# A longer loop body for the edge groups of a graph network: 44 groups per iteration in place of 16

## The chip, the cores and the metric

The kernel runs on one core of one Trainium2 chip. The metric is device time in microseconds (us) of one execution. TensorE (PE), VectorE (DVE), ScalarE (ACT), GpSimd (POOL) and SyncE (SP) each run their own instruction stream, with semaphores between them, and each stream is written with its own copy of the loops below.

## The reference

A graph with 2500 nodes of 128 features and 82500 edges, sorted by destination, passes through six layers of a SchNet-like network and then three GIN layers:

```python
for l in range(6):                                   # first network
    W = ssp(edge_attr @ mlp_w1[l] + mlp_b1[l]) @ mlp_w2[l] + mlp_b2[l]
    W = W * C[:, None]                               # C: cosine cutoff of the edge length
    msg = (h @ conv_w1[l])[src] * W
    agg = segment_sum(msg, dst, num_segments=N)
    h = h + (ssp(agg @ conv_w2[l] + conv_b2[l]) @ lin_w[l] + lin_b[l])
x = layernorm(x + h)
for l in range(3):                                   # second network, with x as h
    z = (1 + eps[l]) * h + segment_sum(h[src], dst)
    h = relu(z @ W1[l] + b1[l]) @ W2[l] + b2[l]
out = layernorm(x + h)
```

All in float32; `ssp(x) = softplus(x) - log 2`.

## The kernel before, in words

Edges are put into 176 groups of 512 (4 tiles of 128). A first part, up to about 1070 us, permutes and transposes the edge records once. Then come the six layers. A layer is `Fori(0, NIT)` with NIT = 11 iterations, and the body of an iteration holds U = 16 groups, written out. On each engine the body is a software pipeline over steps `i`:

- PE at step i: first edge product of group i (L787, `ps_h`); selection of the source rows of group i-2 (L686, `ps_g`, named `ps_a` in the rows) and its second product (L696, `ps_w`); one tile of the neighbour counts that the second network needs (L715); the aggregation of group i-4 (L706, `ps_a`), which waits until DVE has added group i-5 into `aggT`.
- DVE at step i: adds group i-5 into its windows of `aggT` (L1456, four instructions, one after the other), multiplies the message of group i-3 (L1463), finishes the softplus of group i (L1585), and does its share of a count tile (L1495, L1496, L1509).
- ACT at step i: exponential and logarithm of group i (L1075, L1077), copies the selected rows of group i-2 (L1035) and seeds the product bank of group i-1 (L1039).
- POOL: for each group four one-hot matrices (L589, `phot`), two groups behind the aggregation. At the start of an iteration it copies the indices of the whole body (L604, L605).
- SP issues the two DMA loads of a group (`attr`, `select`) four groups ahead.

The steps of a group i-5 to i-1 of an iteration reach back into the groups of the iteration before, so the pipeline doesn't drain between iterations; at steps under 5 this part stands in `If(it > 0)`. Only after the last iteration of a layer a few extra steps drain it, and `late_chunks` updates the nodes.

Nodes are updated in five chunks of 512. `aggT` is complete for a chunk before the layer ends, because edges are sorted by destination, so three chunks are updated early, in iterations EARLY_AT = [5, 8, 9]: the table `early_now` says in which iteration which chunk stands, each engine loads its entry at the start of an iteration (`load_early`, L427), and the parts of the update stand in `If(early_step > 0)` at steps 0 to 3 (PE L720, L725, L731; DVE L1515, L1520, L1528; ACT L1022, L1024, L1029). The other two chunks follow in `late_chunks`.

COUNT_STEP gives the steps at which a count tile is done: 3 to 14, which is BT = 12 tiles in an iteration, or 792 in all; the counts share the banks `ps_t` with the early chunks. `Uses` keeps the registers that the waits compare with.

Of the kernel before, what the change touches and what calls it, by code (L numbers as in the profile page):

```python
# [23 lines left out]
P = 128  # L24
# [16 lines left out]
CHUNKS = 3  # L41
# [12 lines left out]
AS = M  # L54
BG = -(-REAL // (L0 * NIT))
BT = BG * TPG
# [31 lines left out]
ADD_LAG = 6  # L88
COUNT_MAX = 255
# [15 lines left out]

COUNT_STEP = list(range(3, 15))
assert len(COUNT_STEP) == BT


def chunk_of(g):  # L110
    return max(k for k in range(CHUNKS) if GROUP_FIRST[k] <= g)


def gnn_program(nc, xT_d, srcc_d, dst_d, plan_d, ew_d, rec_d, edge_w_d, b2_d, first_w_d, node_w_d, gin_w_d,
# [9 lines left out]
    with ExitStack() as ctx:  # L124
# [25 lines left out]

        early_now = sb("early_now", [P, NIT], i32)
        slack = sb("slack", [P, 1])
# [88 lines left out]
        tile_after = spare[:, 0:PTC * (BLOCKS - 1) // 2 + 1].bitcast(bf16)  # L241
        pends, plan = spare[:, 4 * GE:4 * GE + 2 * PT], spare[:, 7 * GE:7 * GE + NG + NIT]
        assert 2 * PT <= 3 * GE and NG + NIT <= GE
        prel_now = sb("prel_now", [P, U * TPG])
# [168 lines left out]
        def turned_after(r):  # L413
# [11 lines left out]

        def load_early(eng, it, least=0):
            return eng.value_load(early_now[0:1, bass.ds(it, 1)], min_val=least, max_val=EARLY)  # L427

# [200 lines left out]
        def _(pe):  # L629
# [147 lines left out]
            with pe.Fori(0, L0) as layer:  # L777
                prime(layer)
                with pe.Fori(0, K) as k:
                    with pe.Fori(0, NIT) as it:  # L780
                        uses = Uses(pe, layer * (K * NIT) + k * NIT + it).ready(-1, -5)
                        early_step = load_early(pe, it)
                        for i in range(U):
                            if i == 0:
                                uses.wait_attr(i)
                                uses.wait(ssp_done, i - 2)
                            pe.matmul(ps_h[i % 2][:, :], edge_w[0:G1, EW_W1:EW_W1 + F], attr[:, i % AS, :],  # L787
                                      start=True, stop=True).then_inc(mm1_done[i % M], 1)
                            if i >= 2:
                                second_product(uses, it, i - 2, layer)  # L790
                            else:
                                with pe.If(it > 0):
                                    second_product(uses, it, i - 2, layer)
                                if i == 1:
                                    with pe.If(k * NIT + it < 1):
                                        keep_turning(FILL_FIRST)
                            if i == 3:
                                with pe.If(early_step > 0):
                                    chunk_project(layer * NCH + load_early(pe, it, 1))
                            for q in tiles_at(i - 1):  # L800
                                count_tile(uses, q)
                            if i + 1 < U:
                                uses.wait_attr(i + 1)
                                uses.wait(ssp_done, i - 1)
                            if i >= 4:
                                aggregate(uses, i - 4)
                            else:
                                with pe.If(it > 0):
                                    aggregate(uses, i - 4)
                            if i == 0:  # L810
                                with pe.If(early_step > 0):
                                    early = load_early(pe, it, 1)
                                    pe.wait_ge(node_w_in, layer * 16 + 16)
                                    uses.wait(add_done, -1 - ADD_LAG)
                                    uses.wait_count(count_added[TPG - 1], -1)
                                    chunk_prod1(pe.snap(early * CH - CH), layer * NCH + early)
                            if i == 2:
                                with pe.If(early_step > 0):
                                    chunk_prod2(layer * NCH + load_early(pe, it, 1))
                    uses = Uses(pe, layer * (K * NIT) + k * NIT + (NIT - 1))  # L820
# [153 lines left out]
        def _(act):  # L974
# [80 lines left out]
            with act.Fori(0, L0) as layer:  # L1055
# [4 lines left out]
                with act.Fori(0, K) as k:  # L1060
                    with act.Fori(0, NIT) as it:
                        uses = Uses(act, layer * (K * NIT) + k * NIT + it)
                        uses.ready(-1, -5)
                        early_step = load_early(act, it)
                        for u in range(U):
                            if u == 1:
                                with act.If(early_step > 0):
                                    chunk_softplus(layer * NCH + load_early(act, it, 1))
                            if u == 3:
                                with act.If(early_step > 0):  # L1070
                                    early = load_early(act, it, 1)
                                    chunk_store(act.snap(early - 1), layer * NCH + early,
                                                act.snap((layer * EARLY + early + (EARLY - 1)) * 16), next_half)
# [119 lines left out]
        def _(dve):  # L1193
# [215 lines left out]
            for g in range(GROUP_FIRST[CHUNKS - 1], GROUPS):  # L1409
# [18 lines left out]
            steps.sync()  # L1428
            dve.tensor_scalar(early_now[:, :], plan[:, NG:NG + NIT], sorted_dst[:, :], None, ALU.mult
                              ).then_inc(early_set, 1)  # L1430
# [126 lines left out]
            with dve.Fori(0, L0) as layer:  # L1557
# [4 lines left out]
                with dve.Fori(0, K) as k:  # L1562
# [4 lines left out]
                    with dve.Fori(0, NIT) as it:  # L1567
# [3 lines left out]
                        counted = dve.snap(layer * NIT + it)  # L1571
                        early_step = load_early(dve, it)
                        for i in range(U):
                            if i >= 5:
                                add_window(uses, i - 5, it)
# [5 lines left out]
                            if i >= 3:  # L1581
# [5 lines left out]
                                                     ).then_inc(ssp_done[i % M], 1)  # L1587
                            if i == 0:
                                with dve.If(early_step > 0):
                                    chunk_clamp(layer * NCH + load_early(dve, it, 1))  # L1590
                            if i == 1:
                                with dve.If(early_step > 0):
                                    chunk_ssp(layer * NCH + load_early(dve, it, 1))
                            if i == 2:
                                with dve.If(early_step > 0):
                                    early = load_early(dve, it, 1)
                                    chunk_h(dve.snap(early * CH - CH), layer * NCH + early)
                                window_ready(layer * K + k)
# [174 lines left out]
```

## Time and profile before

| what | value |
|---|---|
| median of 3 runs | 5893.71 us (5890.15 to 5894.4) |
| the profiled execution's own time | 5894.77 us |
| its span, first to last instruction | 5893.1 us |
| mean granted TensorE clock | 0.919 |
| busy: PE, DVE, ACT, POOL | 83%, 60%, 47%, 68% |

Times in the rows count from the start of the span. A digit of the engine rows is the busy share of a slice of 147 us in tenths. The layers fill the slices 8 to 38, and in these PE is nearly always busy; the second network follows after 5560 us.

### The profile page before, as it was taken

Reading aid. Unit: us, or ns where it says so; the run is one execution under the profiler, and the core shown is the slowest. Engines: PE = TensorE matmul, PEld = TensorE weight load, DVE = VectorE, ACT = ScalarE, POOL = GpSimd, SP = SyncE. Lnnn points to the kernel's source line nnn. Section 1 sums busy time; section 2 is a strip of 40 time slices with the busy share of each in tenths; the row PEclk is TensorE's granted clock in tenths of the full one; section 3 lists DMA queues with packets and bytes.
Section 4 is the critical chain, followed back from the end, with each engine's and each line's share of the span. In section 5 each row is a group of like instructions: output and inputs, shape, how many; then the busy total and the mean of one; then the engine's idle time right before and its main releaser. Section 6 shows DMA issues by size and latency. Waiting matters only on the chain.

```text
span 5893.1 us, 130525 instructions
## 1 busy us (share of the span) xinstructions
PE 4903.4 (83%) x33026; PEld 3993.5 (68%) x33041; DVE 3560.8 (60%) x10645; ACT 2777.2 (47%) x4801; POOL 4011.3 (68%) x5030
## 2 busy tenths in 40 slices
PE   1036446899999999999998999999999999999999
PEld 0035446777777777777777777877778777777644
DVE  8412224576666766667676666766667667666522
ACT  0012223455555555555555555555555555555422
POOL 4777773577776777767777677776777767777500
PEclk5567778999999999999999999999999999999999
DMA  8258667533333333333333333434333343333200
GB/s 344 77 167 277 213 218 242 165 123 117 119 119 119 124 119 118 119 120 123 120 122 116 119 120 119 124 117 120 121 119 122 117 122 123 118 121 118 90 2 10
DMA packets 431082, 778.19 MB, mean 132 GB/s; under 512 B 55099, under 2 KB 115973, under 8 KB 427349
## 3 DMA queue, kind: packets, MB, share of 16 engines
q1 hardware_dynamic: 388108, 728.55, 38.9%
q0 software_dynamic: 20640, 34.39, 1.8%
q10 hardware_dynamic: 21928, 11.64, 0.7%
q14 instruction: 371, 3.03, 0.2%
q8 instruction: 35, 0.57, 0.0%
HBM read 605.57 MB, written 168.79 MB: 131 GB/s over the span
## 4 chain that ended last, share of the span: by engine, by line
PE 57%; issue 13%; POOL 11%; DVE 9%; DVEq 6%; DMA 1%; ACT 1%; SPq 1%; ACTq 0%; POOLq 0%
PE ps_a L706 14%; PE ps_a L686 12%; PE ps_w L696 12%; PE ps_h L787 12%; POOL permuted L571 11%; DVE aggT L1456 6%; DVEq L333 3%; PE ps_pair L905 3%; DVEq L1456 1%; DVE src_hot L1495 1%; DVEq L427 1%; DVE hid L1585 1%; DVEq L1509 1%; PE ps_pair L720 1%; DVE counts L1509 1%
## 5 line engine op out<-in xcount | busy, mean ns | idle before, releaser
L589 POOL TENSOR_SCALAR phot<-pwin_now,prel_now,pcut_now 128x128 f32<-128x128 f32 x4224 | 3298.7, 796 | 1021.2 <-PE ps_a L706 985.6
L1456 DVE TENSOR_TENSOR aggT<-aggT,ps_a 128x128 f32 x4224 | 1212.8, 287 | 888.0 <-issue 367.0
L686 PEld LDWEIGHTS ps_a<-hi_mid,buffers 128*128 128x128 f32 x8448 | 1127.7, 195 | 575.8 <-issue 575.1
L706 PE MATMUL ps_a<-phot,ex_msg 128*128 128x128 f32 x8448 | 1204.7, 287 | 276.7 <-DVE aggT L1456 276.0
L706 PEld LDWEIGHTS ps_a<-phot,ex_msg 128*128 128x128 f32 x8448 | 1053.9, 196 | 342.0 <-issue 330.5
L1075 ACT ACTIVATE xc<-ps_h 128x512 f32<-128x512 f32 x1056 | 630.4, 597 | 1278.3 <-PE ps_h L787 1265.1
L686 PE MATMUL ps_a<-hi_mid,buffers 128*128 x8448 | 1143.2, 279 | 30.7 <-ACT hid L1035 27.9
L787 PE MATMUL ps_h<-buffers,edge_w 112*128 112x512 f32 x2112 | 1136.7, 621 | 7.7 <-DVE hid L1585 7.7
L696 PE MATMUL ps_w<-edge_w,hid 128*128 128x128 f32 x8448 | 1120.3, 276 | 0.0
L696 PEld LDWEIGHTS ps_w<-edge_w,hid 128*128 128x128 f32 x8448 | 1034.4, 193 | 0.0
L1585 DVE SCALAR_TENSOR_TENSOR hid<-xc,ps_h 128x512 f32<-128x512 f32 x1056 | 722.8, 684 | 335.7 <-PE ps_w L696 267.9
L571 POOL DMA_INDIRECT permuted<-counts x645 | 653.8, 1014 | 248.4 <-issue 195.9
L1039 ACT COPY ps_w<-seed_rows 128x512 f32<-128x512 f32 x1056 | 624.4, 591 | 398.0 <-DVE ex_msg L1463 395.5
L1077 ACT ACTIVATE xc<-xc,half_col 128x512 f32<-128x512 f32 x1056 | 762.3, 722 | 34.7
L1463 DVE TENSOR_TENSOR ex_msg<-ps_w,hid 128x512 f32<-128x512 f32 x1056 | 721.8, 684 | 12.0 <-issue 11.7
L1035 ACT COPY hid<-ps_a 128x512 f32<-128x512 f32 x1056 | 598.7, 567 | 26.5 <-PE ps_a L686 26.3
L668 PE MATMUL ps_h<-ident_lane,hid 128*104 128x128 f32 x1408 | 217.4, 304 | 459.6 <-DMA hid<-permuted 459.3
L668 PEld LDWEIGHTS ps_h<-ident_lane,hid 128*104 128x104 f32 x1408 | 187.7, 191 | 476.2 <-DMA hid<-permuted 289.8
L787 PEld LDWEIGHTS ps_h<-buffers,edge_w 112*128 112x128 f32 x2112 | 336.6, 198 | 48.6 <-issue 42.5
L1016 ACT COPY ex_msg<-ps_h 104x512 f32<-104x512 f32 x88 | 51.6, 586 | 586.8 <-PE ps_w L672 586.8
L1395 DVE COPY buffers<-hid 128x4 f32<-128x4 f32 x176 | 43.4, 246 | 422.5 <-DMA hid<-permuted 408.4
L1509 DVE TENSOR_TENSOR counts<-counts,ps_pair 128x128 f32 x792 | 223.6, 282 | 61.6 <-issue 61.4
(236 smaller groups left out, 2875.6 us busy)
## 6 DMA issues: line engine op xcount, KB each, us to landing
buffers<-src_select SPq DMA_DIRECT2D x1056, 256.0 KB, 2.8
buffers<-attr_permuted SPq DMA_DIRECT2D x1056, 224.0 KB, 2.8
hid<-permuted SPq DMA_DIRECT2D x176, 208.0 KB, 4.3
counts<-in_rec SPq DMA_DIRECT2D x19, 1404.0 KB, 9.9
permuted<-aggT SPq DMA_DIRECT2D x26, 944.0 KB, 26.8
src_select<-ex_msg SPq DMA_DIRECT2D x88, 256.0 KB, 4.8
src_select<-buffers SPq DMA_DIRECT2D x88, 256.0 KB
attr_permuted<-ex_msg SPq DMA_DIRECT2D x88, 224.0 KB, 3.6
```

Source lines behind the costliest of these rows:

```text
L571: pool.indirect_dma_start(out=perm_d[:, :], out_offset=bass.IndirectOffsetOnAxis(ap=pos_i[:, t:t + 1], axis=0), in_=rec[:, r % RING, t - P ...
L589: op = pool.tensor_scalar(phot[:, u % 2, t, :], pwin_now[:, :], prel_now[:, u * TPG + t:u * TPG + t + 1], pcut_now[:, u * TPG + t:u * TPG ...
L686: mm = pe.matmul(ps_g[:, t * F:(t + 1) * F], select[:, u % AS, t * P:(t + 1) * P], table[:, bass.ds(starts[t], F)], start=True, stop=True)
L696: mm = pe.matmul(ps_w[u % 2][:, t * F:(t + 1) * F], hid[:, u % 2, t * P:(t + 1) * P], edge_w[:, EW_W2:EW_W2 + F], start=False, stop=(t == ...
L706: mm = pe.matmul(ps_a[:, t * PWIN:(t + 1) * PWIN], msg[:, u % 2, t * F:(t + 1) * F], phot[:, u % 2, t, :], start=True, stop=True)
L787: pe.matmul(ps_h[i % 2][:, :], edge_w[0:G1, EW_W1:EW_W1 + F], attr[:, i % AS, :], start=True, stop=True).then_inc(mm1_done[i % M], 1)
L1039: act.copy(ps_w[v % 2][:, :].rearrange("p (t f) -> p t f", f=F), seed_rows[:, :].unsqueeze(1).broadcast_to([P, TPG, F])).then_inc(seeded[v ...
L1075: act.activation(xc[:, u % 2, :], ps_h[u % 2][:, :], ACT.Exp).then_inc(exp_done, 1)
L1077: act.activation(xc[:, u % 2, :], xc[:, u % 2, :], ACT.Ln, bias=half_col[:, :]).then_inc(log_done, 1)
L1456: dve.tensor_tensor(window, window, ps_a[:, t * PWIN:(t + 1) * PWIN], ALU.add).then_inc(part_added[t] if t < TPG - 1 else add_done[u % M], 1)
L1463: dve.tensor_tensor(msg[:, u % 2, :], ps_w[u % 2][:, :], picked[:, u % 2, :], ALU.mult).then_inc(msg_done[u % M], 1)
L1585: dve.scalar_tensor_tensor(out=hid[:, i % 2, :], in0=xc[:, i % 2, :], scalar=LOG_MAX, in1=ps_h[i % 2][:, :], op0=ALU.min, op1=ALU.max).the ...
```

## The change

The body holds 44 groups and a layer has 4 iterations: 176 groups as before. What hangs on these two numbers:

- Iterations in the whole program: 24 in place of 66. POOL's copies of the indices are 176 columns wide in place of 64.
- The early chunks stand at "spots", one at step 0 and one at step 22 of the body (SPOT = 22), so a layer has 8 of them. EARLY_AT becomes [3, 6, 7]: chunk 0 at step 22 of iteration 1, chunk 1 at step 0 of iteration 3, chunk 2 at step 22 of iteration 3; that is at the groups 66, 132 and 154 of the layer, where it was 80, 128 and 144. PE, DVE and ACT load their entry of `early_now` at each spot.
- The count tiles stand at the steps 4 to 21 and 26 to 39: 32 in an iteration, 768 in all. A layer's padding of tiles is smaller (NG 192 in place of 198).

```diff
-U = 16
+U = 44
-NIT = 11
+NIT = 4
-BG = -(-REAL // (L0 * NIT))
+BG = -(-GROUPS // (L0 * NIT))
-EARLY_AT = [5, 8, 9]
+SPOT = 22
+SPOTS = U // SPOT
+EARLY_AT = [min(s for s in range(NIT * SPOTS) if chunk_of(max(0, s * SPOT - ADD_LAG)) >= k) + n for k, n in ((1, 0), (2, 0), (2, 1))]
-COUNT_STEP = list(range(3, 15))
+COUNT_STEP = [step for step in range(U) if 4 <= step % SPOT and step < U - 1][:BT]
...
-        early_now = sb("early_now", [P, NIT], i32)
+        early_now = sb("early_now", [P, NIT * SPOTS], i32)
...
+        def counted_until(step):
+            return sum(at < step for at in COUNT_STEP) // TPG
...
 (PE; DVE and ACT in the same way)
-                        early_step = load_early(pe, it)
                         for i in range(U):
+                            if i % SPOT == 0:
+                                spot = pe.snap(it * SPOTS + i // SPOT)
+                                early_step = load_early(pe, spot)
...
-                            if i == 3:
+                            if i % SPOT == 3:
                                 with pe.If(early_step > 0):
-                                    chunk_project(layer * NCH + load_early(pe, it, 1))
+                                    chunk_project(layer * NCH + load_early(pe, spot, 1))
...
-                            if i == 0:
+                            if i % SPOT == 0:
                                 with pe.If(early_step > 0):
...
-                                    uses.wait(add_done, -1 - ADD_LAG)
-                                    uses.wait_count(count_added[TPG - 1], -1)
+                                    uses.wait(add_done, i - 1 - ADD_LAG)
+                                    uses.wait_count(count_added[TPG - 1], counted_until(i) - 1)
...
-                            if i == 2:
+                            if i % SPOT == 2:
```

## Rows read from the trace of the kernel before

**Rows 1.** The page: span, busy times, PE and its clock by slices.
```profile
span 5893.1 us, 130525 instructions
PE 4903.4 (83%) x33026; PEld 3993.5 (68%) x33041; DVE 3560.8 (60%) x10645; ACT 2777.2 (47%) x4801; POOL 4011.3 (68%) x5030
...
PE   1036446899999999999998999999999999999999
...
PEclk5567778999999999999999999999999999999999
```

**Rows 2.** Windows, third layer, iterations: length, busy (count) per engine, PEclk, DMA.
```profile
2697.75:2762.80 65.05, 60.52 (x429) 51.34 (x428) 45.19 (x135) 37.11 (x64) 50.38 (x66) 0.97 0.39 122
...
3027.88:3092.81 64.93, 60.69 (x430) 51.29 (x429) 45.20 (x135) 37.22 (x64) 50.38 (x66) 0.97 0.39 122
3092.81:3162.85 70.04, 63.98 (x441) 52.64 (x441) 47.76 (x139) 38.95 (x67) 50.40 (x66) 0.98 0.38 117
```

**Rows 3.** Windows inside the iteration at 3027.88, from group to group.
```profile
3027.88:3035.60 7.72, 3.99 (x27) 3.17 (x27) 2.36 (x7) 2.29 (x4) 3.12 (x4) 1.00 0.42 129
3035.60:3040.79 5.19, 5.19 (x29) 4.16 (x27) 2.44 (x7) 2.49 (x5) 3.12 (x4) 0.68 0.01 2
3040.79:3044.33 3.54, 3.54 (x29) 3.06 (x27) 2.51 (x9) 2.28 (x4) 3.12 (x4) 1.00 0.43 139
...
3047.87:3051.51 3.64, 3.64 (x29) 3.15 (x28) 2.92 (x10) 2.28 (x4) 3.64 (x5) 1.00 0.43 135
3051.51:3055.54 4.03, 3.83 (x29) 3.15 (x28) 2.87 (x9) 2.27 (x4) 3.23 (x5) 1.00 0.37 126
```

**Rows 4.** Chain that ended last, the same boundary: start, us, what.
```profile
3027.96 3.18 issue
3031.13 0.06 DVEq L1567
```

**Rows 5.** Timeline, the same boundary: start, us, what [idle before <-releaser].
```profile
3032.93 1.55 DVE L1456 TENSOR_TENSOR aggT<-aggT,ps_a 128x128 f32 x4 [4.97 <-issue]
...
3034.62 1.19 PE L706 MATMUL ps_a<-phot,ex_msg 128*128 128x128 f32 x8 [3.73 <-DVE aggT L1456]
3035.60 1.92 PE L787 MATMUL ps_h<-buffers,edge_w 112*128 112x512 f32 x2
...
3040.79 1.02 PE L787 MATMUL ps_h<-buffers,edge_w 112*128 112x512 f32 x2
```

**Rows 6.** DMA queues in the gap 3027.5:3031.1: packets, MB, share.
```profile
q14 instruction: 1, 0.01, 0.5%
```

**Rows 7.** DMA queues, 680:1064 (first part, no loops).
```profile
q8 instruction: 14, 0.23, 0.2%
```

**Rows 8.** DMA queues, 1070.66:1133.6, the first iteration of the first layer.
```profile
q8 instruction: 5, 0.08, 0.6%
```

**Rows 9.** DMA queues, 1830:5560, layers two to six: every instruction packet.
```profile
q14 instruction: 279, 2.29, 0.2%
```

**Rows 10.** Windows: straight code of 680:1064; eleven groups of layers one and three.
```profile
680.00:1064.00 384.00, 234.24 (x1688) 211.63 (x1688) 138.51 (x761) 113.83 (x212) 206.70 (x201) 0.82 0.75 245
...
1092.18:1133.60 41.42, 40.85 (x300) 34.68 (x298) 32.49 (x100) 25.50 (x44) 34.36 (x44) 1.00 0.41 132
2588.10:2629.50 41.40, 40.86 (x300) 34.88 (x299) 32.08 (x98) 26.20 (x46) 32.26 (x42) 1.00 0.43 133
```

**Rows 11.** Timeline, an early chunk at an iteration's start.
```profile
3171.21 1.92 PE L720 MATMUL ps_pair<-aggT,node_w 128*128 x2
...
3181.47 1.07 PE L725 MATMUL ps_pair<-ex_msg,node_w 128*128 128x512 f32 x2
```

**Rows 12.** Loads of the early entry, line 427: ns min/median/max.
```profile
L427 PEldq TENSOR_LOAD <-early_now x126: 308/313/674, 1067.4 to 5557.9; - x126
```

**Rows 13.** Timeline, POOL after the boundary at 3027.88.
```profile
3045.39 4.68 POOL L589 TENSOR_SCALAR phot<-pwin_now,prel_now,pcut_now 128x128 f32<-128x128 f32 x6 [0.44 <-POOL pcut_now L605]
```

**Rows 14.** Timeline, DVE at the second layer's start.
```profile
1831.27 0.15 DVE L1559 TENSOR_SCALAR cb_ln<-node_w 128x1 f32<-128x1 f32 x1 [5.73 <-DMA node_w<-in_node_w]
```

More of the change, by code:

```diff
@@ L81, with chunk_of @@
 STEP_PRIME = 5
-EARLY_AT = [5, 8, 9]
+ADD_LAG = 6
+def chunk_of(g):
+    return max(k for k in range(CHUNKS) if GROUP_FIRST[k] <= g)
+SPOT = 22
+SPOTS = U // SPOT
+assert SPOTS * SPOT == U
+EARLY_AT = [min(s for s in range(NIT * SPOTS) if chunk_of(max(0, s * SPOT - ADD_LAG)) >= k) + n for k, n in ((1, 0), (2, 0), (2, 1))]
 EARLY = len(EARLY_AT)
@@ L1063, in _ @@
                         uses.ready(-1, -5)
-                        early_step = load_early(act, it)
                         for u in range(U):
-                            if u == 1:
+                            if u % SPOT == 0:
+                                spot = act.snap(it * SPOTS + u // SPOT)
+                                early_step = load_early(act, spot)
+                            if u % SPOT == 1:
                                 with act.If(early_step > 0):
-                                    chunk_softplus(layer * NCH + load_early(act, it, 1))
-                            if u == 3:
+                                    chunk_softplus(layer * NCH + load_early(act, spot, 1))
+                            if u % SPOT == 3:
                                 with act.If(early_step > 0):
-                                    early = load_early(act, it, 1)
+                                    early = load_early(act, spot, 1)
                                     chunk_store(act.snap(early - 1), layer * NCH + early,
@@ L1428, in _ @@
             steps.sync()
-            dve.tensor_scalar(early_now[:, :], plan[:, NG:NG + NIT], sorted_dst[:, :], None, ALU.mult
+            dve.tensor_scalar(early_now[:, :], plan[:, NG:NG + NIT * SPOTS], sorted_dst[:, :], None, ALU.mult
                               ).then_inc(early_set, 1)
@@ L1587, in _ @@
                                                      ).then_inc(ssp_done[i % M], 1)
-                            if i == 0:
+                            if i % SPOT == 0:
                                 with dve.If(early_step > 0):
-                                    chunk_clamp(layer * NCH + load_early(dve, it, 1))
-                            if i == 1:
+                                    chunk_clamp(layer * NCH + load_early(dve, spot, 1))
+                            if i % SPOT == 1:
                                 with dve.If(early_step > 0):
-                                    chunk_ssp(layer * NCH + load_early(dve, it, 1))
+                                    chunk_ssp(layer * NCH + load_early(dve, spot, 1))
+                            if i % SPOT == 2:
+                                with dve.If(early_step > 0):
+                                    early = load_early(dve, spot, 1)
+                                    chunk_h(dve.snap(early * CH - CH), layer * NCH + early)
                             if i == 2:
-                                with dve.If(early_step > 0):
-                                    early = load_early(dve, it, 1)
-                                    chunk_h(dve.snap(early * CH - CH), layer * NCH + early)
                                 window_ready(layer * K + k)
@@ L1739 @@
     rec = np.ascontiguousarray(attr.reshape(EACH, P, REC).transpose(1, 0, 2))
-    plan = np.zeros((P, NG + NIT), np.float32)
-    for c, it in enumerate(EARLY_AT):
-        plan[:, TILE_FIRST[chunk_of(it * U - ADD_LAG)] // TPG:NG] = (c + 1) * CH
-        plan[:, NG + it] = c + 1
+    plan = np.zeros((P, NG + NIT * SPOTS), np.float32)
+    for c, spot in enumerate(EARLY_AT):
+        plan[:, TILE_FIRST[chunk_of(spot * SPOT - ADD_LAG)] // TPG:NG] = (c + 1) * CH
+        plan[:, NG + spot] = c + 1
     w1 = np.zeros((L0, P, F), np.float32)
```

19 lines of the change are left out of this document (9 added, 10 removed).

## The prediction

> **What bounds the kernel now.** I read the page first [rows 1]. PE is at 9 tenths or more in all slices of the six layers, at nearly its full clock, so a layer ends when PE has done its groups. Then I cut one layer into iterations [rows 2]. An iteration without an early chunk takes 65.05 or 64.93 us and PE is busy for 60.5 to 60.7 us of it: some 4 us are lost somewhere. The windows from group to group [rows 3] say where. In steady state a group takes 3.54 us, 3.64 us with a count tile, and 4.03 us at every fourth count tile, where DVE also loads the places of the next four. These windows are filled by PE. Only the first two groups of the body are long: 7.72 and 5.19 us.
>
> The chain of waits [rows 4] and the timeline [rows 5] show why. DVE's loop branch (L1567) is followed by 3.18 us in which its sequencer does nothing that is recorded; its next work, the addition of the last group but four into `aggT`, starts 4.97 us after its last instruction. PE waits 3.73 us for that addition before L706. Afterwards PE runs its next matmuls slower: the pair L787 takes 1.92 us in place of 1.02, and the granted clock of that window is 0.68, which is a mix of the two levels 2.4 and 1.2 GHz; in the idle time before, it was still granted 1.00 [rows 3, 5]. So a boundary costs PE twice, by the wait and by a slow stretch behind it. In the gap lies exactly one instruction packet of queue q14 [rows 6]: DVE is fetching code.
>
> The Trainium skill ("Runtime: NRT & Kernel Launch", Instruction fetch mechanics) says that a taken branch out of the loaded window forces a fetch before execution goes on. By that rule, the trace agrees.
>
> **What a boundary costs, and what goes.** Sixteen steady groups would take 16 x 3.54 = 56.6, plus 12 x 0.10 for count tiles = 1.2, plus 3 x 0.38 for the places = 1.1: 59.0 us. The iteration takes 64.9 to 65.0, so a boundary costs 5.9 us; by the other way, 7.72 + 5.19 - 2 x 3.54 = 5.8 [rows 3]. I take 5.8. A layer has 10 boundaries now and 3 afterwards: 7 x 6 = 42 go, 42 x 5.8 = 243.6 us. Nothing else is late in its place in mid-body: POOL needs 3.12 us a group and DVE is busy 2.51 us of 3.54 [rows 3]. The price stays the same at the 18 that remain, as far as DVE makes it; others are below.
>
> **Count tiles.** 792 become 768: 24 x 0.10 + 6 x 0.38 = 4.7 us less, since each stands on PE's or DVE's full path [rows 3]. No end far away: nothing to 5 us.
>
> **Early chunks.** At a boundary one costs 70.04 - 65.0 = 5.0 to 5.5 us [rows 2]. In it PE's own work is three products: the first took 1.92 us at the slow clock, the second 1.07 at full clock [rows 11], the third is of the same size as one of a group's, 0.9. At full clock that is 2.9 us, the lower bound at mid-body. The rest is DVE, which takes four more instructions of 512 columns and at a body's step 3 already starts counting. At step 22 PE comes in at full clock, and the first count tile stands at step 26, a step later than now. I take 4.2 there, between 2.9 and 5.5. Of 18 chunks 12 move to a mid-body spot: 12 x 1.2 = 14 us less; the 6 at a boundary gain 0.4 each from the later count tile, 2 us. Together 16 us less, between 0 and 36.
>
> **What the mid-body spots add.** At step 22 PE, DVE and ACT each load an entry: 313 ns on PE's sequencer [rows 12] and some ALU work and branches, 0.6 to 0.7 us together. They are no engine work; PE's sequencer loads four starts for each group in the same way and the group still takes 3.54 us. DVE has over 1 us of air at steps 22 to 25, which have no count tile. Twelve spots without a chunk at 0.3 us: 4 us; bounds 0 and, where all of it shows, 0.7 x 24 = 17 us.
>
> **POOL's copies.** 176 columns in place of 64, on an engine that sits idle at the boundary anyway: POOL starts its first new group at 3045.39 [rows 13], 3.12 us of work, and PE wants it near the end of step 4, at about 3050.5 (step 5 starts at 3051.51 and an aggregation takes 1 us) [rows 3]. That is 2 us of air; nothing.
>
> **Code fetch of the longer body, the one thing that grows.** Queue q8 brings PE's code: 14 packets in straight code in which PE ran 1688 matmuls and as many weight loads [rows 7, 10], so 241 of these per packet of 16 KB. In the first iteration of the first layer it brings 5 [rows 8], and in the layers two to six none at all [rows 9]: the only instruction packets there are q14's. So PE's whole layer is resident now. The new body has 429 x 2 x 44/16 = 2360 such instructions, 10 packets, and with the sequencer's own some 12. Whether that still fits no row shows.
>
> (The skill's same section gives PE's instruction memory as 128 KiB or 2048 instructions. By it the new body does not fit, and PE must fetch at each loop branch as DVE does; this speaks against the change.)
>
> Since no row decides it, I take the dearer case, not fitting, from PE's side with DVE's price. First, fetching in a straight line: in the first layer's first iteration PE received its packets while it ran; eleven groups there took 41.42 us, the same eleven in the third layer, without a fetch, 41.40 [rows 10]. So it costs nothing. Second, the loop branch: if PE loses what DVE loses, 3.2 us or, as its packets are twice as long, 4 us, its first three products of the new body (2.9 us at full clock) start 4 us later, at 3032. They end at 3035 to 3036.5, where L706 starts at 3034.62 now [rows 5]; the slow stretch that follows today would lie in front. So the two fetches overlap nearly whole. I add 0.5 us for each of 18 boundaries, 9 us, bounds 0 and 3.5 each (63). ACT's body grows likewise; it has over 1 us of idle time in every group and its first product of the new body comes from PE. SP issues its loads four groups ahead, 14 us. At a layer's start DVE waits 5.73 us for the node weights [rows 14], and PE's branch lies under it: 0.5 us x 6 = 3, bounds 0 and 3 each (18).
>
> **Sum.** -243.6 - 4.7 - 16 + 4 + 9 + 3 = -248 us against the profiled execution's own 5894.8 us (1.1 us over the median): 5646.5; against the median of 5893.7, **5645 us**. Preparation and second network stay.
>
> **The rivals.**
> - *Fetches add up* (18%): PE, ACT or POOL come back from the loop branch later than DVE, and L706 waits for PE's own products or, further on, for `phot`. For it: four engines now leave their loaded window at once, and POOL's air is 2 us only. Against: the overlap above. With 3 us more at 18 boundaries and 1 at each layer: 5645 + 60 = 5705.
> - *The mid-body spot stalls like a boundary* (5%): the skip over the early block leaves DVE's window. For it: nothing but the price of 5.8 us; against: three such skips at steps 0 to 2 stand in every iteration now and steps 2 and 3 take 3.54. 24 x 5.8 = 139: 5784.
> - *The other side: PE's straight fetch doesn't keep up* (4%). Twelve packets in each of 24 iterations, 288 in all, and a packet takes 0.6% x 62.9 us x 16 engines / 5 = 1.2 us of an engine [rows 8]. If PE stood still for each, 288 x 1.2 = 346 us: 5990, slower than before. It decides from 0.86 us per packet. Against: the two equal stretches of rows 10.
> - *It doesn't do what it says* (2%): the 5.8 us belong to something that comes every 16 groups, not to the branch. For it nothing; at 5895.
> - The forecast: 71%, its own range 5610 to 5690.
>
> Faster than 5882 (0.2%, about what can be told from no change): 71 + 18 + 5 = 94%, same 2%, slower 4%. The range: below, early chunks at the bound and no price for PE's branch give 5645 - 20 - 12 = 5613, and a cheaper boundary 5605; above, it takes in the first rival with its bound, 5720.
>
> **What would show it.** In the profile after, six layers of 3 boundaries each: iterations of about 168 us (44 x 3.54 + 32 x 0.10 + 8 x 0.38 = 162.0, plus 5.8). L706's wait for L1456 falls to under half. Queue q8 has some 250 packets more, spread over the layers, and steady groups still take 3.54 and 3.64 us; if they take longer, the third rival is right. The window over step 0 and 1 tells the first rival: over 15 us in place of 12.9, with PE's own sequencer late. A gap at step 22 of an iteration without a chunk tells the second. The forecast is wrong if the boundaries that are left cost over 9 us each, or if the groups lose 0.1 us each (106 us in all).

## The result, and the profile after

| | before | after |
|---|---|---|
| median | 5893.79 us (4 runs) | 5767.03 us (5763.99 to 5768.43, 4 runs) |
| ratio | 1 | 0.9785, 95% interval 0.9772 to 0.9799 |
| preparation, to the first product of layer one | 1070.7 us | 1076.3 us |
| six layers, each from its first to its last group's first product (L787, after: L797) | 4319.1 us | 4145.1 us |
| five transitions between these | 153.3 us | 195.9 us |
| what follows | 350.1 us | 349.3 us |

The change is worth 127 us, half of the 248 that were forecast. The layers give 174 us; the transitions take back 43. The 5.6 us more of preparation lie wholly ahead of the layers: PE enters its layer loop at 1072.1 us in place of 1066.6. In the runs below on chips with this preparation, PE enters it between 1065.3 and 1071.7 us, in no order of the body's length, so no run puts these 5.6 us down to the change.

The page after, with the busy times and the queues that carry instructions (packets, MB, share):

```profile
span 5766.7 us, 127153 instructions
...
PE 4825.2 (84%) x33002; PEld 3960.9 (69%) x33017; DVE 3537.8 (61%) x10489; ACT 2763.3 (48%) x4801; POOL 3985.2 (69%) x4946
...
q8 instruction: 374, 6.13, 0.4%
q14 instruction: 403, 3.30, 0.2%
```

Queue q8, PE's code, had 35 packets in the page of before. It now has 374, and in layers two to six, where there was none [rows 9]:

```profile
q8 instruction: 283, 4.64, 0.5%
q14 instruction: 301, 2.47, 0.3%
```

The layer is cut again from each group's first product to the next one's, and a group is called by its step in the body. Windows of the third layer (length, busy and count of PE, PEld, DVE, ACT, POOL, then PEclk, DMA share, GB/s): three iterations; the two windows of a boundary and the group behind it; step 22 without an early chunk; step 22 with one:

```profile
2535.08:2703.32 168.24, 159.79 (x1126) 132.90 (x1126) 116.85 (x342) 100.17 (x174) 131.18 (x170) 0.98 0.40 126
2703.32:2882.89 179.57, 168.96 (x1189) 143.09 (x1189) 126.21 (x367) 103.49 (x179) 137.46 (x178) 0.97 0.40 124
2882.89:3053.89 171.00, 162.58 (x1177) 138.80 (x1177) 123.80 (x364) 101.56 (x176) 137.48 (x178) 0.98 0.41 129
2694.08:2703.32 9.24, 3.51 (x26) 2.84 (x25) 3.31 (x9) 2.28 (x4) 6.22 (x8) 0.92 0.40 114
2703.32:2709.55 6.23, 6.22 (x26) 5.19 (x27) 1.57 (x3) 2.40 (x4) 0.00 (x0) 0.57 0.01 4
2709.55:2713.09 3.54, 3.54 (x28) 3.06 (x27) 2.38 (x6) 2.28 (x4) 3.11 (x4) 1.00 0.49 141
2965.79:2970.54 4.75, 3.83 (x29) 3.15 (x28) 2.87 (x9) 2.26 (x4) 3.11 (x4) 1.00 0.48 136
2787.20:2793.20 6.00, 4.96 (x32) 3.62 (x30) 2.96 (x9) 2.38 (x4) 3.97 (x6) 1.00 0.55 167
```

The steady group still takes 3.54 us, with q8's packets running beside it. The boundary takes 9.24 + 6.23 in place of 7.72 + 5.19 [rows 3]. Its long windows are now those of the old body's last group and the new body's first, one group earlier, since PE itself now stops, before the new body's first product. The timeline shows it (start, us, what, idle before and its releaser):

```profile
2702.12 1.55 DVE L1468 TENSOR_TENSOR aggT<-aggT,ps_a 128x128 f32 x4 [4.63 <-issue]
...
2703.32 2.08 PE L797 MATMUL ps_h<-buffers,edge_w 112*128 112x512 f32 x2 [5.73 <-issue]
...
2705.19 1.91 PE L694 MATMUL ps_a<-hi_mid,buffers 128*128 x8
...
2709.55 1.02 PE L797 MATMUL ps_h<-buffers,edge_w 112*128 112x512 f32 x2
```

DVE loses about what it lost before (4.63 us, 4.97 in [rows 5]). PE, which had lost only by waiting for DVE, now stands for 5.73 us, waits for nobody, and then runs its next 18 products at about half their pace (1.02 to 2.08, 1.05 to 1.91; clock 0.57 over the window). ACT and POOL wait for PE, and none of SP's loads is waited for.

PE's branches name the place. Durations of the iteration loop's branch and of the layer loop's branch (ns, minimum/median/maximum), in the kernel before:

```profile
L780 PEldq COMPARE_BRANCH  x66: 76/208/222, 1131.9 to 5545.2; - x66
L777 PEldq COMPARE_BRANCH  x6: 67/209/229, 1823.1 to 5570.4; - x6
```

and after:

```profile
L788 PEldq COMPARE_BRANCH  x24: 67/3454/3996, 1238.8 to 5419.4; - x24
L785 PEldq COMPARE_BRANCH  x6: 67/7166/7467, 1796.3 to 5445.3; - x6
```

A loop branch takes PE 3.5 us now, one back to the layer's start 7.2; both rows count the last branch of each loop too, which is not taken and lasts 0.07. As the median of the 18 boundaries, two packets of q8 start 1.0 and 4.6 us after the start of the branch, the branch ends 3.68 us after its start, and the first product comes another 3.57 us later: after the second packet.

The start of the third layer, with `prime` (PE's 16 small products that seed its banks for the first groups; L742, after: L750). Before, there was no idle time in front of it. Now there are 7.17 us; the end of DVE's wait [rows 14] is the second line, and PE's first edge product (L797) comes after it, where it came before it:

```profile
2531.38 3.77 PE L750 MATMUL ps_w<-b_row,ones_row 1*128 1x128 f32 x16 [7.17 <-issue]
...
2532.23 0.15 DVE L1571 TENSOR_SCALAR cb_ln<-node_w 128x1 f32<-128x1 f32 x1 [6.14 <-DMA node_w<-in_node_w]
...
2535.08 3.78 PE L797 MATMUL ps_h<-buffers,edge_w 112*128 112x512 f32 x4
```

And step 22 without a chunk, on DVE and PE:

```profile
2966.45 0.29 DVE L1521 TENSOR_TENSOR counts<-counts,ps_pair 128x128 f32 x1 [0.34 <-issue]
...
2967.88 1.55 DVE L1468 TENSOR_TENSOR aggT<-aggT,ps_a 128x128 f32 x4 [1.14 <-issue]
...
2969.58 1.13 PE L714 MATMUL ps_a<-phot,ex_msg 128*128 128x128 f32 x8 [0.92 <-DVE aggT L1468]
```

DVE's load of the spot's entry (2966.47 to 2967.23 on its sequencer) stands in the 1.14 us ahead of the addition that PE waits for. Just before it (2965.25 to 2966.07) DVE's sequencer has loaded the places of four count tiles.

### The profile page after: what moved, and what is told of

Same layout as the page of the kernel before. It is cut to its first block, busy times and chain, and to the rows that moved or that the text cites. A ratio compares the mean times of both kernels' runs of the same rounds, so it can differ in the third digit from the quotient of the medians.

```text
span 5766.7 us, 127153 instructions
## 1 busy us (share of the span) xinstructions
PE 4825.2 (84%) x33002; PEld 3960.9 (69%) x33017; DVE 3537.8 (61%) x10489; ACT 2763.3 (48%) x4801; POOL 3985.2 (69%) x4946
## 4 chain that ended last, share of the span: by engine, by line
PE 60%; issue 12%; POOL 11%; DVE 8%; DVEq 5%; ACT 1%; DMA 1%; SPq 1%; ACTq 0%; POOLq 0%
PE ps_a L714 14%; PE ps_a L694 13%; PE ps_w L704 13%; PE ps_h L797 13%; POOL permuted L579 11%; DVE aggT L1468 5%; PE ps_pair L915 3%; DVEq L338 3%; DVEq L1468 1%; DVE src_hot L1507 1%; DVE hid L1599 1%; DMA permuted<-aggT 1%; DVEq L1521 0%; POOL counts L586 0%; DVEq L435 0%
## 5 line engine op out<-in xcount | busy, mean ns | idle before, releaser
L714 PE MATMUL ps_a<-phot,ex_msg 128*128 128x128 f32 x8448 | 1175.9, 282 | 94.6 <-DVE aggT L1468 93.5
L797 PE MATMUL ps_h<-buffers,edge_w 112*128 112x512 f32 x2112 | 1111.7, 608 | 101.0 <-issue 100.9
L694 PE MATMUL ps_a<-hi_mid,buffers 128*128 x8448 | 1131.6, 277 | 29.9 <-ACT hid L1045 29.5
L714 PEld LDWEIGHTS ps_a<-phot,ex_msg 128*128 128x128 f32 x8448 | 1035.0, 193 | 149.1 <-issue 140.5
L797 PEld LDWEIGHTS ps_h<-buffers,edge_w 112*128 112x128 f32 x2112 | 330.6, 195 | 130.6 <-issue 129.8
```

Source lines behind the costliest of these rows:

```text
L694: mm = pe.matmul(ps_g[:, t * F:(t + 1) * F], select[:, u % AS, t * P:(t + 1) * P], table[:, bass.ds(starts[t], F)], start=True, stop=True)
L714: mm = pe.matmul(ps_a[:, t * PWIN:(t + 1) * PWIN], msg[:, u % 2, t * F:(t + 1) * F], phot[:, u % 2, t, :], start=True, stop=True)
```

## The experiments

Each has "layers", the sum of the six as in the table above (before 4319.1, after 4145.1), "transitions" (153.3 and 195.9), and the ratio to the kernel before in the same batch. The first four ran on a chip where the preparation took some 1335 us, so only ratios and these sums are compared. The sums, and all means of groups, come from one profiled execution of each kernel.

**Both entries at step 0.** Edit to the kernel after, on PE, ACT and DVE alike:

```diff
-                            if i % SPOT == 0:
-                                spot = pe.snap(it * SPOTS + i // SPOT)
-                                early_step = load_early(pe, spot)
+                            if i == 0:
+                                spots = [pe.snap(it * SPOTS + n) for n in range(SPOTS)]
+                                early_steps = [load_early(pe, at) for at in spots]
+                            spot, early_step = spots[i // SPOT], early_steps[i // SPOT]
```

> The changed kernel (44 groups in the body), but PE, DVE and ACT load both entries of early_now at step 0 of the body; the parts in the If blocks stay where they are. Theory: the 1.2 us that step 22 loses in every iteration (4.75 us in place of 3.54) is DVE's load of the entry, 0.8 us on its sequencer ahead of the addition that PE waits for; at step 0 it lies in the fetch gap. So 24 x 1.2 = 29 us less than the changed kernel's 5767: 5738, and the interval at step 22 back at 3.54 to 3.65. Rival: the loss is in the branches over the early parts, or in DVE's two places of the count tile there; then no change, 5767.

Measured: ratio 0.9751 [0.9734, 0.9767]; layers 4136.1, only 9 us less than after, where 29 were expected; transitions 190.3. Step 22 without a chunk falls from 4.75 to 4.00, first row here, but the boundary grows, its first window to 9.9 us in the median from 9.24:

```profile
3215.93:3219.93 4.00, 3.83 (x29) 3.15 (x28) 2.87 (x9) 2.27 (x4) 3.12 (x4) 1.00 0.37 126
...
2944.74:2954.27 9.53, 3.71 (x28) 3.04 (x27) 2.91 (x9) 2.28 (x4) 6.25 (x8) 0.93 0.43 111
```

So of the 1.21 us of step 22 the load is 0.75. The other 0.46 don't belong to the spot: the steps 6, 10 and 14 take 4.00 us as well, in this kernel and in the kernel after. Each of them, and step 22, holds the product of a count tile (3.65 in place of 3.54) and follows a DVE step in which the places of four tiles are loaded (0.35 more). At the boundary the second entry costs about 0.6 us (8.76 in place of 8.11 us over two steady groups, as a mean), so only 9 us of the 18 (24 x 0.75) stay gained.

**The loop's head shifted.** 64 waits that are long met, merged to 32 instructions, ahead of PE's layer loop, where they run once:

```diff
+            for _ in range(64):
+                pe.wait_ge(perm_kept, GROUPS)
```

> The changed kernel with 32 more instructions (waits that are already met) in PE's straight code ahead of the layer loop, run once. They move PE's loop body against the 16 KB packets of code. Theory: at each loop branch PE now waits for two packets one behind the other, because the body starts a few instructions before a packet's end (packets at 2696.9 and 2700.5, first product at 2703.3). Shifted, one packet is enough: the body's first product comes some 2.3 to 3.3 us earlier after the branch, 18 x 2.5 = 45 us less: 5722. The boundary (last and first interval, 9.2 + 5.9 us) falls from 8.1 us over two steady groups to 5.5 or so. Rival: the second wait is another thing (attr's load, a semaphore); no change but for 1 to 2 us more, 5769.

Measured: ratio 0.9715 [0.9699, 0.9731]; layers 4105.1, 40 us less; transitions 201.8. The same boundary:

```profile
2945.04:2952.38 7.34, 3.70 (x29) 3.04 (x27) 2.44 (x6) 2.28 (x4) 6.22 (x8) 1.00 0.46 143
2952.38:2957.65 5.27, 5.27 (x26) 4.54 (x27) 2.44 (x6) 2.40 (x4) 0.00 (x0) 0.68 0.01 2
```

The branch takes as long (median 3.72 us), the two packets come at the same moments after it (1.0 and 4.7 us), but the first product follows 1.34 us behind the branch in place of 3.57. The boundary costs 7.34 + 5.27 - 7.08 = 5.5 here. The boundaries without a chunk cost 5.5 and 6.1 us (means of the layers' first and of their second): the price of before. Nothing was changed but where PE's code lies in its packets. So the extra price of the 18 boundaries is the wait for the second packet. That the loop's head had only few instructions behind it in the first one is the reading that fits; no trace shows a packet's content.

**Longer bodies.** 88 groups x 2 and 176 x 1; no count tile stands at a spot's last step, and a layer has 120 of them in place of 128 (the padding rounds otherwise):

```diff
-U = 44
+U = 88        (second kernel: 176)
...
-NIT = 4
+NIT = 2        (second kernel: 1)
...
-COUNT_STEP = [step for step in range(U) if 4 <= step % SPOT and step < U - 1][:BT]
+COUNT_STEP = [step for step in range(U) if 4 <= step % SPOT < SPOT - 1][:BT]
```

> U = 88, NIT = 2 (one boundary in a layer in place of three), count tiles at steps 4 to 20 of each 22. Theory: 12 boundaries less than the changed kernel at 8.1 us each, 97 us; layer starts (PE's 7.5 us branch) and the four spots of a layer stay: 5767 - 97 = 5670. Rival (longer code costs in straight line too): at or over 5720.

> U = 176, NIT = 1: the body is the whole layer, no boundary inside. Theory: 18 boundaries less at 8.1 us, 146 us: 5767 - 146 = 5621; PE's branch at the layer's end still takes 7 to 8 us and all 8 spots of a layer still cost. Rival: something grows with the body (registers, fetch in straight line), at or over 5700.

Measured: 88 groups 0.9597 [0.9581, 0.9613], layers 4030.7, transitions 197.3; 176 groups 0.9462 [0.9446, 0.9478], layers 3948.9, transitions 198.9. The first step takes 12 boundaries away and 114 us, 9.4 of them by the 48 count tiles less, so 8.8 us each (a few spots cost less here as well, see "Blocks only where a chunk can be"); the second takes the last 6 and 82 us, 13.6 each, of which 9.4 are the boundary and the rest comes from the groups around it and the layers' first. The transitions do not grow with the body any more (195.9, 197.3, 198.9).

**Idle code behind a condition, first try.** In the 16 groups of the kernel before, with 36 idle instructions (`keep_turning`: products whose result nobody uses) and, in the second, 12:

```diff
+                            with pe.If(early_step > EARLY):
+                                keep_turning(36)        (second kernel: 12)
```

> The kernel before (16 groups, 11 iterations) with an If block of 36 filler matmuls in each step of PE's body, behind a condition that never holds (early_step > EARLY). Nothing of it runs; it only makes PE's body some 2300 instructions long, as the 44 groups do, all else as before. Theory: PE's body is no longer resident, so queue q8 brings code in every iteration (some 9 packets of 16 KB), PE's loop branch waits for it at 60 boundaries and at 5 layer starts. The boundary rises from 5.8 us to 7 to 8.5, a layer's start by 8 us: +70 to +160 and +45: 1.02 to 1.035 of before. Steady groups stay at 3.54 and 3.65. Rival (what grew in the change is not PE's code but the longer body's other work): same time as before, q8 silent.

> As b1_pe_code_2300, with 12 fillers in each block: PE's body is some 1600 instructions, the layer's code with its ends some 2300. Theory: the body stays resident within a layer, the layer's start does not: boundaries as before (5.8 us), layer transitions longer by 8 us each: +45 us, 1.007 of before. q8 some 3 to 9 packets a layer. Rival: a body that fits keeps all: 1.000.

Measured: 1.0003 [0.9994, 1.0013] and 1.0005 [0.9996, 1.0015]. That tells nothing of the theory: q8 brought 35 packets in all, as many as before, so PE's program had its old length. The condition lies outside the value's declared range, and the compiler must have dropped the blocks.

**A short body.** The kernel before with 8 groups x 22, two count tiles a step at steps 3 to 6:

```diff
-U = 16
+U = 8
...
-NIT = 11
+NIT = 22
...
-EARLY_AT = [5, 8, 9]
+EARLY_AT = [9, 16, 17]
...
-COUNT_STEP = list(range(3, 15))
+COUNT_STEP = [3, 3, 4, 4, 5, 5, 6, 6]
```

> The kernel before with U = 8, NIT = 22: eight groups in the body, 21 boundaries in a layer, early chunks in iterations 9, 16 and 17, count tiles two at a step at steps 3 to 6 (1056 tiles). DVE's body is half as long. Theory: a boundary's 5.8 us are DVE's code fetch; half the body is at most two or three packets of 8 KB and stays, q14 falls silent within the layers, a boundary costs 1 to 2 us. 126 x 1.5 in place of 60 x 5.8, and 264 count tiles more at 0.2: 190 - 348 + 53 = -105 us: 0.982 of before. Rival (the branch itself, or the pipeline's refill, costs): 66 x 5.8 + 53 = +436 us, 1.07.

Measured: 1.042 [1.0403, 1.0438], layers 4539.7; 0.982 was expected. First group, steady group, a group with two tiles, last group:

```profile
3033.51:3038.09 4.58, 3.98 (x26) 3.15 (x27) 2.31 (x7) 2.27 (x4) 2.68 (x4) 1.00 0.04 12
3038.09:3041.63 3.54, 3.54 (x28) 3.06 (x27) 2.46 (x7) 2.40 (x5) 3.13 (x4) 1.00 0.34 128
...
3052.42:3057.04 4.62, 3.89 (x31) 3.25 (x29) 3.50 (x14) 2.33 (x5) 3.29 (x4) 1.00 0.45 131
3061.79:3067.25 5.46, 4.05 (x30) 3.22 (x28) 4.08 (x15) 2.49 (x5) 3.70 (x5) 1.00 0.40 128
```

Queue q14, DVE's code, from 1900 to 5500 us:

```profile
q14 instruction: 20, 0.16, 0.0%
```

It had 269 packets in the same stretch of before. So DVE's body of 8 groups stays loaded, and the boundary costs 1.04 us, at most 1.9 if all that the last group has over a group with two tiles is its too, in place of 5.8. The branch and the pipeline's refill are still there, and q14's packets and most of the price are gone: the 5.8 us are the fetch of DVE's code, and behind it PE's start at the slow clock. The kernel is slower for another reason, which the expectation had at 0.2 us a tile: two tiles in a group cost up to 1.1 us, five times what two groups with one tile pay.

**The next entry loaded early.** The kernel of 176 groups, with each spot's entry loaded 18 steps ahead:

```diff
+                            if i % SPOT == 4 and i + SPOT < U + 4:
+                                next_spot = pe.snap(it * SPOTS + i // SPOT + 1)
+                                next_step = load_early(pe, next_spot)
```

> U = 176, NIT = 1 with the entry of the next spot loaded at step 4 of each 22, so no load stands at a spot. Theory: 42 spots in mid-body lose 0.75 us less each, as the first experiment on the entries gave (4.75 to 4.00): 31 us less than a4_u176, 0.5% of before: 0.941. Rival: the load only costs elsewhere, 0.946.

Measured: 0.9449 [0.9433, 0.9464], 5563.02 us; layers 3944.9. The layers take four us less than with the load in its place, where 31 were expected: step 22 lost its 0.7 us, other groups gained 0.3 to 0.5. The rival is right.

**PE's code alone made longer.** The kernel before, with blocks that never run but can't be dropped; DVE's, ACT's and POOL's code is untouched:

```diff
+                            with pe.If(K > 2):
+                                keep_turning(36)        (second kernel: 12)
```

> The kernel before (bodies of 16 groups, 11 iterations), with 36 idle TensorE instructions behind a condition on K that is never met at run time in each of the 16 groups of the body: they are in the program and never run. PE's body then has about as many instructions as the body of 44 groups (some 2300), while DVE's, ACT's and POOL's stay as they were. Theory (PE's code no longer stays loaded, and it pays at each taken branch, in two packets of q8 at a loop branch): q8 brings packets in all six layers, a boundary costs 7 to 8.5 us in place of 5.8 (60 of them: +70 to +160) and each layer's start 8 us more (5 of them and the first, +40): ratio 1.02 to 1.035. Rival (the dearer boundary of the long body comes from DVE's, ACT's or POOL's longer code): 0.998 to 1.003, even if q8 brings packets. If the skips themselves cost, the steady group is over 3.54 us and tells it.

> The same with 12 idle instructions behind the condition in each group in place of 36: PE's loop body grows by about 200 to 400 instructions and may still fit, while body, layer's start and layer's end together are longer than in the kernel before. Theory: layers are entered at the dear price if q8 brings packets there (5 to 6 times 8 us: +45, ratio 1.007) and boundaries stay at 5.8 us. Rival: all still stays loaded, no q8 packets in layers two to six, ratio 0.999 to 1.001.

Measured with 36: 1.03 [1.0283, 1.0317]; layers 4441.4, 122 us more than before, which is 2.0 for each of 60 boundaries; transitions 199.3, 46 more. The steady group stays at 3.54, so skipping the blocks costs nothing. The branch of the iteration loop, q8 in layers two to six, and a boundary with the group behind it:

```profile
L780 PEldq COMPARE_BRANCH  x66: 76/3548/3986, 1131.8 to 5714.6; - x66
```

```profile
q8 instruction: 590, 9.67, 1.1%
```

```profile
2827.68:2836.68 9.00, 3.81 (x29) 3.13 (x27) 3.19 (x11) 2.28 (x4) 6.25 (x8) 1.00 0.40 115
2836.68:2841.97 5.29, 5.29 (x26) 4.26 (x27) 2.25 (x6) 2.40 (x4) 0.00 (x0) 0.68 0.01 3
2841.97:2845.51 3.54, 3.54 (x28) 3.06 (x27) 2.37 (x6) 2.29 (x4) 3.12 (x4) 1.00 0.40 146
```

Measured with 12: 1.0074 [1.0057, 1.0091]; layers 4314.5, not above before; transitions 200.6, 47 more. Its loop branch, q8, and what PE waits for at the third layer's start:

```profile
L780 PEldq COMPARE_BRANCH  x66: 76/208/212, 1132.0 to 5589.5; - x66
```

```profile
q8 instruction: 45, 0.74, 0.1%
```

```profile
PE ps_w L742 <- issue: 7.8, 1, 7.8
```

Both effects of the change are here, each by itself, in the kernel before and with no other engine's code touched. With 36 the body no longer stays loaded: boundaries go from 5.92 to 7.97 us, and layer starts up by 9 us (the branch of the layer loop takes 8.2 us as the median of five). With 12 the body stays, the way from a layer's end to its start does not: q8's 45 packets lie at the layers' ends, at their starts and in their first 50 us, and only the 9 us at the starts are paid. The rival, another engine's code, is out for both.

**Blocks only where a chunk can be.** 176 groups, entry loads and conditions at spots 3, 6 and 7 alone:

```diff
+def has_early(i, step):
+    return i % SPOT == step and (NIT > 1 or i // SPOT in EARLY_AT)
...
-                            if i % SPOT == 0:
+                            if has_early(i, 0):
```

> The body of a whole layer (176 groups, 1 iteration), in which the entry loads and the blocks of an early chunk stand only at the three spots that have one, in place of all eight. Theory: a spot without a chunk costs 0.75 us for the load and 0.3 us for the skips where the steps are full; five such spots in each of six layers go: 15 to 30 us less in the layers than with all eight (3948.9 us over the six layers, ratio 0.946), ratio 0.941 to 0.944. Rival: with a load that meets slack further on the cost moves and does not go: within 6 us of 3948.9.

Measured: 0.9448 [0.9433, 0.9464]; layers 3945.3. The rival is right. Of the five spots taken away three (0, 22, 110) had cost 0.6 to 0.7 us each and two (44 and 88) nothing; and some 0.36 us each came back at steps 6, 18 and 81. The run with 176 groups and all eight spots shows what sets 22 and 44 apart. Its windows of the third layer, steps 22 and 44, both with an entry's load and no chunk:

```profile
2813.09:2817.63 4.54, 3.78 (x29) 3.14 (x27) 2.39 (x7) 2.01 (x4) 3.12 (x4) 1.00 0.48 143
2894.70:2898.24 3.54, 3.54 (x28) 3.06 (x27) 2.66 (x8) 2.49 (x5) 3.12 (x4) 1.00 0.42 144
```

Steps 22 and 110 follow a load of four tiles' places on DVE, steps 44 and 88 don't. The same load of an entry costs 0.7 us in the first case and nothing in the second.

**PE's first products ahead of the branch.** The same, and `prime` for the next layer at the end of this one:

```diff
+            prime(0)
             with pe.Fori(0, L0) as layer:
-                prime(layer)
...
+                with pe.If(layer < L0 - 1):
+                    prime(layer + 1)
```

> As the run before in this batch, and PE issues the first products of the next layer's window (prime) at the end of a layer, ahead of the layer loop's branch, in place of behind it. Theory: the 7.5 us that PE's branch takes at a layer's start lie in the path from one layer's last product to the next one's first; with prime ahead of it 3 to 4 us of PE's own work are done before the code arrives: transitions 3 to 4 us shorter each (5 of them, 199 us in sum now), 15 to 20 us in all, another 0.003 of the ratio. Rival: the transition is set by DVE's part (node weights, second network of the layer) and PE's branch lies beside it: no change.

Measured: 0.9461 [0.9445, 0.9477]; transitions 182.0, 17.4 less, as expected; layers 3961.9, 16.6 more. The first is what the theory said; the time as a whole doesn't change, as the rival said, but not for its reason: ahead of the third group PE runs its filler products and doesn't wait for DVE. At the third layer's start:

```profile
2465.49 2.07 PE L803 MATMUL ps_h<-buffers,edge_w 112*128 112x512 f32 x2 [6.50 <-issue]
2468.72 2.07 PE L803 MATMUL ps_h<-buffers,edge_w 112*128 112x512 f32 x2 [1.17 <-issue]
2470.59 4.50 PE L763 MATMUL ps_a<-still,ones_mat 128*128 128x512 bf16 x14
```

L803 comes 3.5 us sooner (17.4 / 5), where `prime` stood. But now the slow clock, which `prime`'s short products had taken on themselves, falls on it and on the filler products L763 (4.50 us in place of 3.23), and the first two groups take 0.9 and 1.4 us more than in the run before (2.8 and 6.3 in place of 1.9 and 4.8). Against the run before, 5572.8 to 5565.2 us, nothing is gained.

## Why the prediction was half right

| term | forecast, us | measured, us |
|---|---|---|
| 42 boundaries go | -243.6 | -244.0 (42 x 5.81) |
| PE's fetch at the 18 that stay | +9 | +41.4 (18 x 2.30) |
| PE's fetch at layer starts | +3 | +35.1 |
| spots at mid-body | +4 | +18.0 (24 x 0.75) |
| early chunks | -16 | +13.0 |
| count tiles and their places | -4.7 | +5 |
| preparation and second network | 0 | +4.8 |
| sum | -248 | -127; the two spans differ by 126.4 |

Prices are means over the six layers, from group to group, above 3.54 us. A boundary without a chunk takes 5.92 before, of which 0.11 is a count tile's product in its first window, so 5.81; after, where no tile stands there, it takes 8.11. The layer starts are 42.6 in the transitions, less 7.5 by which the first four groups of the layers are shorter. A spot's 0.75 is step 22's 1.21 less the 0.46 of its count tile and places, which stand in the line of the count tiles: 162 us after, 157 before. That line comes out above zero since step 30 takes 4.36 us in place of 4.00 (24 x 0.36 = 9); why, no run shows.

*What held.* The price of a boundary, nearly to the digit, and its cause (the short body shows it from the other side), that it goes with the branch, the steady groups at 3.54 and 3.65, PE's fetch in a straight line at no cost, no stall in the skip over the early block (step 44 of 176 takes 3.54), POOL's copies at nothing (with the head shifted the boundary costs 5.8 as before). So the two rivals at 5784 and 5990 were wrong in mechanism, though 5784 is the nearest number to the result; that nearness is luck.

*What failed first: "the loop branch ... the two fetches overlap nearly whole. I add 0.5 us".* The sketch had PE come back 4 us after its branch with its code. The branch does take 3.5 to 3.7 us, and with the head shifted, the overlap was as drawn and the price zero (5.79 us a boundary, 5.81 before). But in the kernel after, PE had to wait for a second packet, 3.6 us behind the first. I had a packet's content (241 products and loads) and not where in a packet the loop's head lies; one packet was taken for granted. My bound of 3.5 us each did hold the 2.30; the rival "fetches add up" was the right mechanism at boundaries, at 41 in place of 54 us, and its sign is there: the two windows take 15.5 us in place of 12.9, with PE's own sequencer late.

The Trainium skill ("Runtime: NRT & Kernel Launch", Instruction fetch mechanics) has a taken branch out of the window force a fetch of the target page before execution goes on. By that rule the trace agrees, for the first packet; the second one, which decided here, is not in it.

*What failed second: "At a layer's start DVE waits 5.73 us for the node weights, and PE's branch lies under it: 0.5 us x 6", bounds 0 and 3.* Both this error and the one before are 32 us. DVE's wait did lie beside the branch, but PE's branch takes 7.2 us there, double that of a boundary: q8's packets start only 3.4 us after it (2526.95 for the branch at 2523.55), in a stretch where ACT issues the stores of the node table (2523.68 and 2524.86) and SP its loads. And PE's `prime` then runs at the slow clock, 3.77 us in place of 2.05. The first edge products, which don't wait for the node weights, come that much later. I had given the branch the same price everywhere, with DVE's as the model. Whether the later start of the packets is due to these transfers was not tried.

*Third: the mid-body spots, "DVE has over 1 us of air at steps 22 to 25, which have no count tile".* I took 0.3 us, with 0.7 as the bound, which was the right number. The cost is DVE's: 0.75 us of load on its sequencer stand ahead of the one addition PE waits for. And step 22 is not free of count tiles: the places of four are loaded just ahead of it and the last one's addition comes in it. Where no places are loaded there (steps 44 and 88 of the body of 176), the load of an entry is free, as I had thought. The engine work of a step was not the measure, its sequencer's was. It was 12 spots without a chunk in my sum; the 12 with one pay the same.

*Fourth: early chunks, 4.2 us at mid-body.* They take 6.1 and 6.5 us above a spot without one, and 5.45 at a boundary where they took 5.30 before: an error of 29 us. At mid-body the first two groups of a chunk take 1.5 us more than without it (5.99 + 3.82 in place of 4.75 + 3.54), at a boundary after the change 0.75 (8.86 in place of 8.11): part of a chunk lies in the gap that is there anyway. The row of 5.0 to 5.5 us was a price net of that cover, and I took it as the upper bound of a price without it. The lower bound, PE's three products alone, left out what PE waits for: in the chunk at 2787.20 it stands 0.7 us for one of DVE's additions into `aggT`, beyond the 0.9 that a spot without a chunk has too, and 1.7 us for ACT's copy of the selected rows, which comes late behind the chunk's own copy. No run tried the chunks apart.

## What to carry to other kernels

Ask for every engine, not only for the one that stalls now, whether its loop body stays loaded: the instruction queues by stretch show it, a queue that is silent in the later iterations means resident code, and a longer body can end that for an engine that paid nothing so far. The gain of fewer boundaries is then counted against the new price of each that is left and of the outer loop's, which is entered by a longer way; here the best was to have no inner loop at all (0.946, and 0.945 with blocks only where a chunk can be). A load into a register, and any price read off at a stall, must be costed again at its new place: what a gap covered before is bare in the middle of the body. And it must be costed against what the same sequencer does in that step: the same load was free in one step and cost 0.7 us in another.

## What the runs showed of the hardware that I had not expected

- PE's code: a body that fits is not fetched again, one that doesn't makes the loop's branch 3.5 us long in place of 0.21 (medians), and there is a state between: 12 idle instructions a group more left the inner branch at 0.208 us and made the start of each layer 9 us dearer.
- Where the target of a branch lies matters: 32 instructions ahead of the loops, which run once, were worth 40 us in the layers (18 boundaries at 5.8 in place of 8.1 us).
- Packets of q8 are 16 KB (4.64 MB in 283) and behind a loop branch come one after the other, the second 3.6 us after the first; those of q14 are 8 KB (2.47 MB in 301).
- An idle PE comes back at the slow clock even where the granted clock in the gap is still 0.92 or 1.00 (its first two products take 1.92 us [rows 5] and 2.08 us in place of 1.02); which product stands first then decides who pays for it.
